# Two attentions with feed-forward layers on one core: POOL instead of ACT makes the normalised rows of x in the last heads

## The reference

```python
x = x + L0_xattn(layernorm(x), ctx)   # 16 heads of 96, 4 key/value heads, keys from context and x
x = x + L0_ffn(layernorm(x))          # up/relu^2/down, a routed low-rank part, layer norm
x = x + L1_xattn(layernorm(x), ctx)   # 32 heads of 128, 8 key/value heads
x = x + L1_ffn(layernorm(x))          # x W + b, and a low-rank part with a softmax mix
layernorm(x) = (x - mean(x)) / sqrt(var(x) + 1e-5)
```

## Time and profile before

| | |
|---|---|
| median of 3 runs | 1126.47 us (1125.64 to 1127.51) |
| the profiled execution | 1127.2 us, span 1125.4 us |
| busy, share of the span | PE 97%, DVE 48%, ACT 47%, POOL 34% |
| granted clock of PE | 0.996 of full speed over the span |
| last head of the first attention | about 300 to 371 us |
| last head of the second attention | about 1029 to 1088 us |

### The profile page before, as it was taken

The page is one execution under the profiler, slowest core; times in us unless marked ns, Lnnn a source line. Parts: engine busy times, 40 slices in busy tenths (PEclk is TensorE's granted clock), DMA queues, the critical chain, the costliest instruction groups (busy, mean ns, idle before and its releaser), DMA issues.

```text
span 1125.4 us, 14699 instructions
## 1 busy us (share of the span) xinstructions
PE 1094.7 (97%) x5302; PEld 889.8 (79%) x5302; DVE 545.8 (48%) x1004; ACT 534.0 (47%) x1478; POOL 377.8 (34%) x260
## 2 busy tenths in 40 slices
PE   5999999999999999999999999999999999999997
PEld 4888888887877688877888888888888888888775
DVE  4464366357477532484524435344353352533654
ACT  5475366357477432455616336254262442623741
POOL 3053034025252543476404215033050240512441
PEclk9999999999999999999999999999999999999999
DMA  8111001010000321102021021110210202101002
GB/s 250 24 47 30 1 29 29 1 47 10 1 19 1 103 94 38 38 1 90 25 75 37 4 71 37 64 48 0 75 37 19 93 0 75 37 13 46 15 4 75
DMA packets 31918, 47.88 MB, mean 43 GB/s; under 512 B 19364, under 2 KB 23716, under 8 KB 29188
## 3 DMA queue, kind: packets, MB, share of 16 engines
q1 hardware_dynamic: 31876, 47.33, 13.0%
HBM read 41.02 MB, written 2.10 MB: 38 GB/s over the span
## 4 chain that ended last, share of the span: by engine, by line
PE 89%; ACT 5%; DVE 4%; issue 1%; POOL 1%; DMA 0%; SPq 0%; ACTq 0%; DVEq 0%
PE work L603 15%; PE work L605 14%; PE work L604 14%; PE work L662 8%; PE yb L603 5%; PE yb L604 5%; PE yb L605 5%; PE pt L673 4%; PE ov L603 3%; PE ov L605 3%; PE ov L604 3%; PE pt L605 3%; PE pt L604 3%; PE pt L603 3%; ACT prob L1129 2%; DVE oT_lo L1662 1%
## 5 line engine op out<-in xcount | busy, mean ns | idle before, releaser
L1356 POOL TENSOR_TENSOR prob<-prob,exp_rcp 128x512 f32<-128x512 f32 (+1 forms) x96 | 127.2, 1325 | 534.7 <-DVE exp_rcp L1604 534.7
L1129 ACT ACTIVATE prob<-work,neg_max 128x128 f32<-128x128 f32 (+1 forms) x384 | 149.1, 407 | 65.1 <-DVE neg_max L1629 64.9
L603 PE MATMUL work<-xT_hi,q_hi 128*128 128x512 f32 x416 | 168.1, 404 | 0.4 <-DVE xT_lo L1698 0.4
L605 PE MATMUL work<-xT_hi,q_lo 128*128 128x512 f32 x416 | 164.4, 395 | 0.0
L604 PE MATMUL work<-xT_lo,q_hi 128*128 128x512 f32 x416 | 164.4, 395 | 0.0
L1079 ACT ACTIVATE pT_hi<-pt 128x512 fp32r<-128x512 f32 x128 | 73.8, 602 | 84.4 <-PE pt L673 83.6
L662 PE MATMUL work<-kT,qT 128*128 128x128 f32 (+1 forms) x704 | 112.9, 303 | 0.1
L662 PEld LDWEIGHTS work<-kT,qT 128*128 128x128 f32 (+1 forms) x704 | 102.8, 191 | 11.8 <-issue 0.3
L1662 DVE TENSOR_TENSOR oT_lo<-ov,oT_hi 32x128 fp32r<-32x128 f32 (+2 forms) x160 | 67.4, 421 | 77.7 <-ACT oT_hi L1085 76.4
L1629 DVE TENSOR_REDUCE neg_max<-work 128x4 f32<-128x512 f32 (+1 forms) x96 | 82.8, 863 | 39.7 <-PE work L662 37.8
L1085 ACT ACTIVATE oT_hi<-ov 32x128 fp32r<-32x128 f32 (+2 forms) x160 | 60.2, 376 | 83.7 <-PE ov L605 81.2
(11 more groups left out here) (216 smaller groups left out, 2103.5 us busy)
## 6 DMA issues: line engine op xcount, KB each, us to landing
raw<-in_l_q SPq DMA_DIRECT2D x8, 1024.0 KB, 5.3
raw<-in_l_o SPq DMA_DIRECT2D x8, 1024.0 KB, 4.7
kv_raw<-in_l_kv SPq DMA_DIRECT2D x8, 515.0 KB, 3.4
prob<-vT SPq DMA_DIRECT2D x128, 32.0 KB, 1.8
raw<-in_l_o SPq DMA_DIRECT2D x4, 768.0 KB, 4.3
raw<-in_l_q SPq DMA_DIRECT2D x16, 144.0 KB, 2.7
qT<-in_ctxT SPq DMA_DIRECT2D x4, 512.0 KB, 5.8
x<-in_x SPq DMA_DIRECT2D x2, 1024.0 KB, 10.3
```

The lines of the kernel that those rows point to most:

```text
L603: pe.matmul(dst, l_hi, r_hi, start=first and k == 0, stop=False)
L605: mm = pe.matmul(dst, l_lo, r_hi, start=False, stop=last and k == n - 1)
L1129: e = act.activation(prob[:, i % 2, g * L.keys:(g + 1) * L.keys], s[:, g, :], ACT.Exp, bias=neg_max[:, i % 2, g:g + 1], accum_out=exp_sum[ ...
L1356: pool.tensor_tensor(p, p, exp_rcp[:, b % 2, :].unsqueeze(2).broadcast_to([P, G, L.keys]), ALU.mult)\
```

## The change

`normalise_x` is no longer called on ACT for `N[1]` and `N[3]`. POOL's new `normal_rows` calls `rstd_of`, waits for its own rstd, waits for the buffer where four rows have been made already, and makes the row with one `tensor_scalar`: x minus the mean, times rstd.

```diff
--- before
+++ after
@@ ACT, head @@
-                    if norm is not None and 4 <= i < NB:
-                        normalise_x(norm, i - 4, x[:, i - 4, :])
                     if norm is not None and L.double:
-                        if i >= NB:
-                            normalise_x(norm, i - 4, x[:, i - 4, :])
                         if i >= 5:
                             norm_hi(norm, i - 5)
...
-                    if norm is not None and not L.double and i >= NB:
-                        normalise_x(norm, i - 4, x[:, i - 4, :])
-                        if i > NB:
-                            norm_hi(norm, i - 5)
-                            lin_hi(i - NB - 1)
+                    if norm is not None and not L.double and i > NB:
+                        norm_hi(norm, i - 5)
+                        lin_hi(i - NB - 1)
...
             norm_hi(N[1], 6)
-            normalise_x(N[1], NB - 1, x[:, NB - 1, :])
...
-            normalise_x(N[3], NB - 1, x[:, NB - 1, :])
             norm_hi(N[3], 6)
@@ POOL @@
+            def normal_rows(n, b):
+
+                rstd_of(n, b)
+                pool.wait_ge(n.rstd, b + 1)
+                if b >= n.bufs:
+                    pool.wait_ge(n.t, b - n.bufs + 1)
+                pool.tensor_scalar(xn_buf(n, b), x[:, b, :], mean_var[:, b, 0:1], rstd[:, b:b + 1],
+                                   ALU.subtract, ALU.mult).then_inc(n.xn, 1)
...
                     if norm is not None and b >= 4:
-                        rstd_of(norm, b - 4)
+                        normal_rows(norm, b - 4)
                     normalise(L, S, it, b)
...
                     for b in range(4, NB):
-                        rstd_of(norm, b)
+                        normal_rows(norm, b)
                         if L.double:
                             add_b(b - 4)
```

## The result

| | before | after |
|---|---|---|
| median of 7 runs each | 1126.73 us (1125.55 to 1128.3) | 1123.55 us (1122.65 to 1124.44) |
| ratio | | 0.9972, 95% interval 0.9961 to 0.9983 |
| profiled execution's span | 1125.4 us | 1121.7 us |

The change is faster by 3.2 us, 0.28%, where 4.8 us was forecast. In a second comparison it was 1123.14 us (1122.73 to 1124.4) against 1127.12, ratio 0.997 (0.996 to 0.998).

What follows compares the result with a forecast made beforehand. PE, busy 97% of the span, was taken as the bound, so gains are its ended waits: 2.89 us in the first attention plus 1.93 in the second, 4.82, giving a median of 1121.7 us, range 1119.7 to 1124.6.

Steps and rivals of the forecast that it cites:

- ACT's place in line: Last heads: ACT's three row instructions delay PE; moving them to POOL gains 2.89 us (first attention) and 1.93 us (second).
- The price of a row: One added tensor_scalar on POOL takes 1.04 us, priced from the broadcast row; lower bound 0.54, upper bound 2.6.
- dear rows: Rival: POOL's rows become what PE waits for; at 3.0 us a row nothing gained, at 4.0 net 4.9 slower; chance 0.10.
- The tight place: Second transposes of first attention's last head: POOL has block 1's row in time up to 1.6 us a row.
- "Wrong" sign: Sign against the forecast: PE waits for POOL's vT at second transposes of first attention's last head (row over 1.6 us).
- the bound of t = 2.4: Second attention's last head, block 3: POOL's row is in time for PE up to 2.4 us a row.
- The sum: PE waits ended in both last heads: 2.89 + 1.93 = 4.82 us, giving a median of 1121.7 us.
- half of it: Rival: a row takes 1.6 to 3.0 us; first attention gives back some gain; 1121.7 to 1126.4 us; chance 0.12.
- The first one is dear: Rival: POOL's first tensor_scalar is delayed by 7.0 us; net 1.0 us slower, 1127.5 us; chance 0.08.
- What was put at nothing: Work queued behind POOL's added rows, the normalisation of probabilities and the end's bias additions, was claimed to cost nothing.
- The end: Behind the second attention, four bias additions slide into POOL's 5.87 us idle at no cost; without it up to 4.2 us.

Runs made afterwards that it cites:

- e4: Changed kernel with POOL's row as one broadcast tensor_tensor multiplication (1.04 us), mean subtraction left out; 1120.66 us.
- e8: Changed kernel with POOL's row as a tensor_scalar of one operation, mean subtraction left out; 1121.91 us.
- e7: Changed kernel with every row made twice by POOL, the second time behind the first; 1148.66 us.
- e3: Changed kernel with block 1's row in the first attention made earlier, right behind block 0's row; 1122.17 us, again 1121.48 us.
- e2: Changed kernel with the change in the second attention's last head only, ACT making the first's rows as before; 1125.54 us.
- e1: Changed kernel with the change in the first attention's last head only, ACT making the second's rows as before; 1124.18 us.
- e9: Changed kernel with block 1's row early in first attention; in second, DVE's xT_lo later and POOL's second-half q split behind block 3's row; 1119.94 us.

## Why the prediction was right in direction and short in size

- **ACT's place in line.** Right. The waits that were to go went, in both attentions, and those that were to stay stayed at the forecast size (0.70 for 0.69) or near it (0.53 twice for 0.64). With the row at the assumed 1.04 us (e4) the gain is 725.71 - 722.40 = 3.31 in A and 75.71 - 73.27 = 2.44 in B, for 2.89 and 1.93 forecast. That sum was small by 0.9. 0.3 of it is pT_lo: the wait of 0.59 went whole, not 0.53 of it, and the other two gave 0.2 each, not 0.09, since DVE's reciprocal and its xT_lo overlap in the rows of after. Most of the rest is no wait: PE's busy time over A and B is 790.00 in e4 and 790.85 before. Why the same products took 0.85 less is open.
- **The price of a row.** This step failed: "A tensor_scalar reads one full tensor and two columns, so the broadcast row is the nearest: t = 1.04." It is 2.08, twice that, inside the bound of 2.6 that the same paragraph gave. The nearest row by what is read was not the nearest by what is done to each element: with one operation in place of two (e8) it is 1.58. The sentence against the dear rows, that every elementwise instruction of this size takes 1.0 to 1.3 us, rested on two groups; POOL's split of 128x512 took 1.41 (L1472 before).
- **The tight place.** It was the right one, the second transposes of the first attention's last head, and that "Wrong" sign is what the profile shows. The formula there, 332.17 + 2t - 335.39, gives 0.94 at 2.08; measured against e4 it is 723.91 - 722.40 = 1.51. Missing were POOL's 0.10 of waiting for its own rstd, twice, and the 0.15 from POOL's end to PE's start, 0.35 of the 0.57. In the second attention the bound of t = 2.4 was too wide as well: 0.28 was lost at 2.08, so by this estimate it holds up to 1.8.
- **The sum.** 4.82 less the formula's 0.94 is 3.88, against 3.95 measured in A + B. That it is so close is luck: the gain and the loss were both too small by some 0.9 (in the loss 0.57 in A and 0.29 in B). The time fell to the rival "half of it", whose condition, t between 1.6 and 3.0, was met. The medians gained less than A + B, 3.2, and C, which the sum did not have, is where the profile shows a loss beside them.
- **The other rivals.** "The first one is dear" fell: the first tensor_scalar lasted 2.10 and the others 2.08, with 0.10 ahead of each. The Trainium skill (GPSIMD Engine Reference, Instruction dispatch) has a cost of some 6 us for a first call to freshly loaded code; no such gap stands before the first tensor_scalar. Two like it in size stand around the all-reduce, 5.68 ahead of it and 6.88 behind it here, 5.87 and 7.01 in the earlier trace rows; what fills them no run shows. "Dear rows" as a slower kernel needed t over 3, and t is 2.08. e7, whose two rows of 2.08 stand for t of about 4.2, shows that it would have come, and harder than the 4.9 us that the text gave for t = 4.0: 1148.66 is 22 us above the kernel before. That working had no clock in it and only two late rows, where seven waits for rows came.
- **What was put at nothing.** The normalisation of the probabilities behind the row rightly (e3 delays it to 336.10 at no cost). The end wrongly: "POOL is idle for 5.87 before its next work, more than four times 1.04, so nothing waits" took that idle time for slack. With the change POOL's additions end 2.2 us nearer to the start of C (2.17 ahead of it, 4.39 before), the gap to the all-reduce stays at 5.68, and the all-reduce starts 2.03 late. So the text's "were it not idle" was the true case, and one row of 2.08, not all four, stands on that path. The three prices of a row (e4, e8, after) move the all-reduce to 0.86, 1.49 and 2.03 behind hd, with the gap at 5.62, 5.64 and 5.68. It costs PE up to 1.8 where its clock is 1.00 (e2 against e1), and 0.2 or less at 0.83.

## What to carry to other kernels

An engine that is half idle can still hold up the busiest one by where an instruction stands in its order; look for an early result that waits behind a late one, and move the work, or the place. Where the instruction to be added is not in the trace, price it by what it does per element as well as by what it reads, and test the tightest place at the upper bound before choosing. Idle time in front of an instruction is slack only if the instruction could have started earlier: the 5.87 ahead of the all-reduce had 0.1 to 0.4 to give, as the 5.4 to 5.8 that stay in every kernel with later rows show. And set the end of a yardstick behind everything that the change can delay. When one engine's order is out of the way, read the next: here ACT's, then POOL's and DVE's, then POOL's again, and only with all moved (e9) was the second attention's last head free of waits.

## What the runs showed of the hardware

- On POOL, 128x512 float32 from SBUF, a tensor_scalar with column operands takes 1.58 us with one operation and 2.08 with two; a multiplication of two tensors, one broadcast, takes 1.04 and an addition of two full ones 1.29. The Trainium skill (GPSIMD Engine Reference, Elementwise — side-by-side cycle accounting) has bodies with two input tensors as the dearer ones, and 769 ns for a best case of 512 elements. The measurement decides: reading one tensor was not the cheaper form here.
- An instruction of POOL that waits for POOL's own result starts 0.10 us behind it; PE starts 0.15 behind POOL's row.
- Waits of PE of 1.8 to 5.7 us cost more than they last (e7): 17.9 us more of waits, 25.0 us more of time, with a granted clock of 0.85 to 0.95 behind them.
- From the end of POOL's last addition to the start of its partition all-reduce 5.4 to 5.8 us passed in the eleven executions in which POOL made the rows of the second attention, with the all-reduce's input there 0.9 to 2.1 us earlier. 6.7 to 7.5 us passed behind it, to POOL's next instruction. What fills these gaps is open.
- The stretch behind PE's wait of 0.88 near the end keeps PE busy for 8.1 to 8.3 us in some executions and for 9.7 to 9.8 in others, at a granted clock of 1.00 and of 0.82 to 0.83; one kernel (e3) showed both. What decides it is open.
